# A decoder layer on one core: the first layer of the feed-forward net as rounded products, two couplings laid out by DMA, new call lists

## The chip, the core and the metric

The kernel runs on one core of a Trainium2 chip. A core has five engines with an instruction stream of their own: TensorE (PE in the profile, with PEld for its weight loads), VectorE (DVE), ScalarE (ACT), GpSimd (POOL) and SyncE (SP, here only the issuer of DMAs). They meet at semaphores: an instruction, or the landing of a DMA, raises one, and another engine waits until it has reached a value. The metric is the device time of one execution in microseconds (us), lower is better; the median of the runs is compared.

## What is computed

A decoder layer over 64 sequences of 256 tokens with 256 features, in fp32: a Mamba2 (SSD) mixer, an attention whose queries come from the sequence and whose keys and values come from 120 context rows and the sequence itself, a feed-forward net of three coupled cycles, each followed by a LayerNorm. The arithmetic to follow the change is that of the feed-forward net:

```python
def _coupling_net(h, w1, b1, w2, b2, w3, b3, w4, b4):
    h = _gelu(h @ w1 + b1)
    h = _gelu(h @ w2 + b2)
    h = _gelu(h @ w3 + b3)
    return jax.nn.sigmoid(h @ w4 + b4)
...
def _twist(x):
    o_r, o_i, p_r, p_i = jnp.split(x, 4, axis=-1)
    return jnp.concatenate([p_r, -p_i, -o_r, o_i], axis=-1)
global_context = x.mean(axis=1, keepdims=True)
gf = _global_net(global_context, gc_w1, gc_b1, gc_w2, gc_b2, gc_w3, gc_b3)
out = x
for _ in range(NUM_CYCLES):
    tf = _coupling_net(out, cn_w1, cn_b1, cn_w2, cn_b2, cn_w3, cn_b3, cn_w4, cn_b4)
    combined = 0.7 * gf + 0.3 * tf
    coupling = BASE_COUPLING + adaptive_range * (combined - 0.5) * 2.0
    out = out + coupling * _twist(out)
```

The rest in one line each:

```python
x = _layernorm(x + _L0_attn_ref(x, ...), axis=-1)             # mixer
x = _layernorm(x + _L0_xattn_ref(ctx_1024, x, ...), axis=-1)  # attention, 8 heads of 64
x = _layernorm(x + _L0_ffn_ref(x, ...), axis=-1)              # 256-256-128-64-1 net, three cycles
```

A coupling is one number for each token. The twist mixes features only, so after two cycles of couplings c and d the output is a sum of x, twisted x and sign-changed parts with factors of c, d and the last coupling e. The kernel uses this twice: cycles 1 and 2 apply the net's first layer to x and to twisted x once (`layer(f, 0, 0)` and `twisted(f)`) and then only combine the results, and the output is formed from x2 with the factors of_x, of_tw and of_minus.

## The kernel before

**Stages.** A sequence is 2 x 128 tokens or 2 x 128 features; 128 is the partition count. The work is a software pipeline. In pass p of `for p in range(NSEQ + 2)` the mixer and the start of the attention work on sequence m = p, the rest of the attention on a = p − 1, the feed-forward net on f = p − 2, and projections of sequence m + 1 begin already. There are 66 passes; 62 hold work of all of f, a, m and m + 1.

**Order.** Each engine runs a list of calls written out by hand, one in the prologue and one in the pass: `tensor` (L467 and the list after it), `scalar`, `vector`, `gpsimd`, `sync`. A call emits a few instructions for one sequence and does nothing where the sequence doesn't exist. Nothing is reordered: an instruction whose semaphore hasn't come holds all that follows on its engine. For SP that holds for its waits too: `keep_inv` and `spread_inv` stand between `load_x`, `load_ctx`, `spread_cum` and `store`.

**PSUM.** Eight banks: scores in 1 to 3, a ring of 4 and 5 (transposed probabilities, values, w_o), a ring of 6 and 7 (mixer projections, `glob`, `twisted`), and bank 0 for the feed-forward net.

**Products.** `product3` (L233, its matmul at L239) is the product of operands that were split into a half rounded to F32R and the rest: three rounds, high by high, low by high, high by low; each is one PE instruction for 128 rows of the contraction. The mixer's projections, `q_pair` (12 of 256 columns), `k_tile` (6 of 376) and `v_tile` (6 of 512) use it. A plain fp32 matmul shows as two PE instructions in the trace: `layer(f, 0, 0)` (L480) and `twisted` (L529, L530) have four matmuls each.

**Feed-forward net.** `x2_turn` (PE, L467) transposes x2; ScalarE's `x2_out` copies it to x2T and sums the tokens; `layer(f, cyc, n)` for n = 0 to 3 alternates a product on PE with a gelu or tanh on ScalarE; `cycle(f, cyc)` on VectorE turns the tanh of all tokens, replicated over partitions, into couplings cpl (L1233) and updates h_pre (L1243, L1245), of which the next cycle's gelu is taken. GpSimd's `twist` forms what the second cycle adds. For the output the couplings are needed a second time, with the token on the partition: `layer(f, cyc, 3)` makes them with a two-column product (L500) behind the two products that replicate (L499), and ScalarE takes a tanh of each (L811 and L813); GpSimd's `factors` makes of_x, of_tw and of_minus of them for `out_sum` on VectorE (L1254).

**Attention's division.** `inverse(a, d)` on VectorE makes the inverses of the softmax sums for head group d. SP's `keep_inv(a, d)` (L1600) writes them to DRAM in four DMAs and `spread_inv(a, d)` (L1610) reads them back replicated over 64 partitions into invT in two; `divide(a, d)` (L1193) multiplies oT with it, and `w_o(a, i)` (PE, L455) projects the result.

**Prologue.** `x_low(0)` (L985) is what TensorE's first product waits for; the context of sequence 0 is loaded behind the weights by `load_ctx(0)` (L1617), and its statistics, `context(0)`, come later on VectorE.

## Time and profile before

| | value |
|---|---|
| median of three runs | 3988.45 us (3987.41 to 3992.45) |
| the profiled execution's own time | 3988.01 us |
| its span (first to last instruction) | 3986.1 us |
| mean granted clock of TensorE | 0.988 |
| PE busy | 3893.1 us, 98% |
| ACT busy | 3265.0 us, 82% |
| DVE busy | 3013.3 us, 76% |
| POOL busy | 1700.7 us, 43% |

The time is that of the whole execution, the span that of the recorded instructions in it. "Busy" is the time in which an engine has an instruction under way, summed over the span; DMA issues, branches and semaphore operations are not counted as busy. The granted clock is TensorE's as a share of its upper level. In a timeline each row is a run of like instructions: start, duration until the last of them ends, engine, line, operation and operands. Matmuls overlap, so the duration of a group on TensorE's own time is read from its start to the start of the next row.

### The profile page before, as it was taken

The numbers are of one execution on the slowest core, as the hardware profiler recorded it, in microseconds if no ns is written. First come the engines' busy times: TensorE is split into PE (matmuls) and PEld (weight loads), VectorE is DVE, ScalarE is ACT, GpSimd is POOL, SyncE is SP. The second block draws the span as 40 slices with busy tenths as digits, with TensorE's granted clock in tenths as the row PEclk, the third lists the DMA queues.
The fourth block names the chain that finished last, engine by engine and source line by source line (L and its number), as shares of the span: only waits on it lengthen the run. The fifth ranks groups of instructions, "written<-read, shape, count | busy, mean of one in ns | idle before, by whom it ended". The sixth has DMA issues, their size and how long they took to land.

```text
span 3986.1 us, 75957 instructions
## 1 busy us (share of the span) xinstructions
PE 3893.1 (98%) x25728; PEld 3057.0 (77%) x25728; DVE 3013.3 (76%) x7082; ACT 3265.0 (82%) x7932; POOL 1700.7 (43%) x2824
## 2 busy tenths in 40 slices
PE   5999999999999999999999999999999999999995
PEld 4777777777777777777778777777777777777774
DVE  6777777877877877877777777777778778778763
ACT  4788888888888888888888888888888888888873
POOL 3344444444444444444444443444444444544431
PEclk7999999999999999999999999999999999999997
DMA  3111111211111111111111111111112111112100
GB/s 96 50 41 56 59 41 53 62 41 53 59 43 53 59 44 53 54 49 53 48 55 53 44 59 53 41 57 57 41 53 62 41 53 59 43 53 59 44 30 14
DMA packets 276722, 202.78 MB, mean 51 GB/s; under 512 B 19824, under 2 KB 275568, under 8 KB 276336
## 3 DMA queue, kind: packets, MB, share of 16 engines
q1 hardware_dynamic: 276336, 197.92, 16.4%
q8 instruction: 207, 3.39, 0.4%
q14 instruction: 179, 1.47, 0.1%
HBM read 180.04 MB, written 17.83 MB: 50 GB/s over the span
## 4 chain that ended last, share of the span: by engine, by line
PE 95%; DVE 1%; ACT 1%; issue 0%; POOL 0%; POOLq 0%; DVEq 0%; ACTq 0%
PE psum L239 29%; PE psum L420 10%; PE psum L444 9%; PE psum L430 9%; PE psum L455 6%; PE psum L330 5%; PE psum L487 5%; PE psum L317 5%; PE psum L480 3%; PE psum L493 3%; PE psum L499 2%; PE psum L529 2%; PE psum L530 1%; PE psum L304 1%; PE psum L467 1%; PE psum L363 1%
## 5 line engine op out<-in xcount | busy, mean ns | idle before, releaser
L762 ACT ACTIVATE prob<-psum,nmax 128x376 f32<-128x376 f32 x1024 | 587.9, 575 | 20.5 <-DVE nmax L1165 3.9
L1438 POOL TENSOR_TENSOR Lm<-Lm,G 128x768 f32<-128x768 f32 x256 | 468.4, 1837 | 265.5 <-ACT Lm L699 265.4
L1165 DVE TENSOR_REDUCE nmax<-psum 128x1 f32<-128x376 f32 x1024 | 544.5, 542 | 37.1 <-PE psum L420 28.3
L1428 POOL TENSOR_SCALAR_AFFINE_SELECT Lm<-Lm 128x256 f32<-128x256 f32 x512 | 218.2, 455 | 767.8 <-DMA Lm<-cum_row 767.8
L430 PE MATMUL psum<-ident,prob 128*128 128x128 f32 (+1 forms) x3072 | 490.7, 276 | 3.1 <-ACT prob L762 2.0
L989 DVE SCALAR_TENSOR_TENSOR u<-psum,par,u 128x255 f32<-128x255 f32 (+5 forms) x960 | 449.4, 479 | 34.2 <-ACT u L640 3.6
L420 PE MATMUL psum<-kT,q_sb 64*128 64x376 f32 x2048 | 462.8, 528 | 2.2 <-ACT kT L743 0.5
L430 PEld LDWEIGHTS psum<-ident,prob 128*128 128x128 f32 (+1 forms) x3072 | 366.8, 141 | 91.5 <-issue 61.3
L1184 DVE COPY probT<-psum 128x384 f32<-128x384 f32 x512 | 278.4, 544 | 178.9 <-PE psum L430 178.0
L444 PE MATMUL psum<-probT,V 128*64 128x256 f32 (+1 forms) x3072 | 386.8, 386 | 0.4 <-ACT V L752 0.4
L239 PE MATMUL psum<-x_hi,w_in_hi 128*128 128x256 f32 (+1 forms) x1152 | 350.3, 304 | 22.2 <-DVE x_lo L985 13.0
L772 ACT ACTIVATE probT<-psum 128x384 f32<-128x384 f32 x512 | 250.6, 489 | 94.1 <-PE psum L430 91.7
L239 PE MATMUL psum<-x_hi,w_in_lo 128*128 128x256 f32 (+1 forms) x1152 | 326.3, 283 | 0.0
L239 PE MATMUL psum<-x_lo,w_in_hi 128*128 128x256 f32 (+1 forms) x1152 | 325.4, 282 | 0.0
L444 PEld LDWEIGHTS psum<-probT,V 128*64 128x64 f32 (+1 forms) x3072 | 200.8, 136 | 105.7 <-issue 22.4
L698 ACT ACTIVATE Lm<-Lm,ncum 128x256 f32<-128x256 f32 x512 | 262.8, 513 | 0.8 <-POOL Lm L1428 0.8
L239 PEld LDWEIGHTS psum<-x_hi,w_in_hi 128*128 128x128 f32 (+1 forms) x1152 | 215.0, 187 | 57.2 <-issue 46.8
L420 PEld LDWEIGHTS psum<-kT,q_sb 64*128 64x128 f32 x2048 | 155.0, 185 | 117.5 <-issue 100.6
L804 ACT ACT_TABLE_LOAD x188 | 241.2, 1283 | 3.3
L762 ACT ACT_TABLE_LOAD x187 | 239.9, 1283 | 3.3
L1447 POOL TENSOR_TENSOR g<-xc,gate 128x256 f32<-128x256 f32 x256 | 190.5, 754 | 122.0 <-DVE xc L1083 93.5
L330 PE MATMUL psum<-w_out_sb,g 128*128 128x256 f32 x1024 | 231.7, 380 | 1.7 <-DVE dt_a L1001 1.7
(203 smaller groups left out, 10692.5 us busy)
## 6 DMA issues: line engine op xcount, KB each, us to landing
Lm<-cum_row SPq DMA_DIRECT2D x64, 1024.0 KB, 5.2
Lm<-cum_row SPq DMA_DIRECT2D x64, 512.0 KB, 6.5
invT<-inv_row SPq DMA_DIRECT2D x256, 128.0 KB, 3.0
xT_sb<-in_xT SPq DMA_DIRECT2D x64, 256.0 KB, 2.9
x_sb<-in_x SPq DMA_DIRECT2D x64, 256.0 KB, 3.4
result<-out_sb SPq DMA_DIRECT2D x64, 256.0 KB, 2.2
inv_row<-inv_t SPq DMA_DIRECT2D x512, 1.0 KB
ctx_sb<-in_ctx SPq DMA_DIRECT2D x64, 120.0 KB, 3.2
```

The source lines that it names most:

```text
L239: t = mm(dst, a, b, start=n == 1, stop=n == 3 * KT)
L330: t = mm(banks[b][:, i * D:(i + 1) * D], g[:, c, i * P:(i + 1) * P], w_out_sb[:, c, :], start=c == 0, stop=c == CT - 1)
L420: mm(banks[b][:, 0:NK], q_sb[r, c, i * P:(i + 1) * P], kT[r, c, :], start=True, stop=True).then_inc(p_sc, 1)
L430: t = tr(banks[b][0:m, j * P:(j + 1) * P], prob[:, r, j0:j0 + m], ident[:, :])
L444: t = mm(banks[b][k * HD:(k + 1) * HD, 0:L], V[0:m, j, h * HD:(h + 1) * HD], probT[0:m, (8 * s + h) % HP, j, :], start=j == 0, stop=j == l ...
L698: act(Lm[:, h, 0:L], Lm[:, h, 0:L], ACT.Exp, bias=ncum[:, 0, h:h + 1])
L762: act(prob[:, r, :], b[:, 0:NK], ACT.Exp, bias=nmax[:, n:n + 1], accum_out=psum_row[:, n:n + 1]).then_inc(a_exp, 1)
L772: act(probT[:, (8 * s + 2 * c + k) % HP, :, i * P:(i + 1) * P], b[:, 0:len(JT) * P].rearrange("p (j t) -> p j t", j=len(JT)), ACT.Copy).th ...
L989: stt(u[0:rows, c, d:L], src[:, 0:L - d], prm("conv_w", 4 * c + 3 - d, slice(0, rows)), u[0:rows, c, d:L], ALU.mult, ALU.add).then_inc(don ...
L1165: e.tensor_reduce(nmax[:, n:n + 1], banks[bank_of["sc", s, n]][:, 0:NK], AX.X, ALU.max, negate=True).then_inc(d_max, 1)
L1184: cp(probT[:, (8 * s + 2 * c + k) % HP, :, i * P:(i + 1) * P], b[:, 0:len(JT) * P].rearrange("p (j t) -> p j t", j=len(JT))).then_inc(d_tn, 1)
L1438: tt(pair, pair, G[:, :].unsqueeze(1).broadcast_to([P, 2, TRI]), ALU.mult).then_inc(l_Lm, 1)
```

## The change

Three things are changed.

First, `layer(f, 0, 0)` and `twisted(f)` are products of three rounds, like the mixer's. Their common operand x2T is split once, by a new VectorE call `x2_split(f)`: a cast to x2T_hi and a subtraction to x2T_lo. The weights are split in the prologue (cw1_hi, cw1_lo and the negated cw1_mhi, cw1_mlo). x2T becomes an alias of h_pre, and h_tw is gone: `twist` now works in place in h_a and h_b and waits until cycle 0 has used them.

Second, only cycle 2 makes its coupling in token order by the two-column product. Those of cycles 0 and 1 are brought to c_col by DMA: `keep_c` writes one row of cpl to DRAM, `spread_c` reads it with the token on the partition (128 partitions, 2 elements of 4 bytes each). Both are issued by SP, and `factors` waits for c_in. ScalarE's tanh of all tokens writes cpl itself, so t4 is gone. ctx_sb holds one sequence instead of two, so `load_ctx(s)` waits for all three uses of the sequence before (d_ctx), and the ring of prob tiles has 7 places instead of 8.

Third, all call lists are in another order, the prologue's too. There, `context(0)` is now ahead of `x_low(0)` on VectorE, and ctxT(0), in_z(0, 1) and y_pair(0, 0) move in front of the loop on TensorE.

```diff
 # tensor
             def layer(s, cyc, n):
...
                 if n == 0:
-                    pe.wait_ge(a_f, FA * s + 1)
+                    pe.wait_ge(set_dve, SET_DVE_ALL)
+                    pe.wait_ge(d_x2, 2 * s + 2)
                     for m in range(KT):
-                        for k in range(KT):
-                            t = mm(b[:, m * L:(m + 1) * L], cw1_sb[:, k, m * P:(m + 1) * P], x2T[:, k, :], start=k == 0,
-                                   stop=k == KT - 1)
+                        cs = slice(m * P, (m + 1) * P)
+                        t = product3(b[:, m * L:(m + 1) * L], [cw1_hi[:, k, cs] for k in range(KT)],
+                                     [cw1_lo[:, k, cs] for k in range(KT)], [x2T_hi[:, k, :] for k in range(KT)],
+                                     [x2T_lo[:, k, :] for k in range(KT)])
...
-                    for i in range(TT if cyc < 2 else 0):
-                        mm(b[:, i * P:(i + 1) * P], cw4_row[:, i, :], h3[:, :], start=True, stop=True)
-                    mm(b[:, L:L + TT], h3[:, :], cw4_col[:, :], start=True, stop=True).then_inc(p_f, 1)
+                    if cyc == 2:
+                        t = mm(b[:, 0:TT], h3[:, :], cw4_col[:, :], start=True, stop=True)
+                    else:
+                        for i in range(TT):
+                            t = mm(b[:, i * P:(i + 1) * P], cw4_row[:, i, :], h3[:, :], start=True, stop=True)
+                    t.then_inc(p_f, 1)
...
 # scalar
-                    sc.wait_ge(l_fac, 9 * s)
-                    t = act(t_col[:, cyc, :], src[:, 1, 0:TT], ACT.Tanh, bias=half_b4[:, :], scale=0.5)
-                    if cyc < 2:
-                        t = act(t4[:, :], src[:, 0, :], ACT.Tanh, bias=half_b4[:, :], scale=0.5)
+                    if cyc == 2:
+                        sc.wait_ge(l_fac, 8 * s)
+                        t = act(t_col[:, :], src[:, 0, 0:TT], ACT.Tanh, bias=half_b4[:, :], scale=0.5)
+                    else:
+                        sc.wait_ge(c_out[cyc], 16 * s)
+                        sc.wait_ge(l_tw, 2 * s)
+                        t = act(cpl[:, cyc, :], src[:, 0, :], ACT.Tanh, bias=half_b4[:, :], scale=0.5)
...
 # vector
+            def x2_split(s):
+                if not live(s):
+                    return
+                ve.wait_ge(a_f, FA * s + 1)
+                ve.wait_ge(p_f, FP * (s - 1) + 2)
+                ve.wait_ge(p_tw, s)
+                cp(x2T_hi[:, :, :], x2T[:, :, :]).then_inc(d_x2, 1)
+                ve.wait_ge(d_x2, 2 * s + 1)
+                tt(x2T_lo[:, :, :], x2T[:, :, :], x2T_hi[:, :, :].bitcast(F32), ALU.subtract).then_inc(d_x2, 1)
...
+            context(0)
             x_low(0)
...
+            split(cw1_raw, cw1_hi, cw1_lo)
...
 # sync
+            def keep_c(s, cyc):
...
+                sp.wait_ge(d_f, FD * s + 3 * cyc + 1)
+                sp.wait_ge(c_in[cyc], 16 * (s - 1))
+                e.dma_start(c_row[s % 2, cyc:cyc + 1, :], cpl[0:1, cyc, :]).then_inc(c_out[cyc], 16)
+
+            def spread_c(s, cyc):
...
+                sp.wait_ge(c_out[cyc], 16 * (s + 1))
+                sp.wait_ge(l_fac, 8 * s)
+                e.dma_start(c_col[:, cyc, :], c_row[s % 2, cyc, :].rearrange("(i p) -> p i", p=P),
+                            allow_slow_non_contiguous=True).then_inc(c_in[cyc], 16)
...
             for p in range(NSEQ + 2):
                 f, a, m = p - 2, p - 1, p
+                load_ctx(m + 1)
                 load_x(m + 1)
-                load_ctx(m + 1)
+                spread_cum(m + 1)
                 keep_inv(a, 0)
+                keep_inv(a, 1)
+                keep_c(f, 1)
+                keep_c(f, 0)
+                spread_inv(a, 1)
+                spread_c(f, 0)
+                spread_c(f, 1)
                 spread_inv(a, 0)
-                spread_cum(m + 1)
-                keep_inv(a, 1)
-                spread_inv(a, 1)
                 store(f)
```

The part of TensorE's new list on which the prediction works, from `twisted(f)` to the end of the pass, with twelve calls between `layer(f, 1, 3)` and `w_o(a, 0)`:

```python
layer(f, 0, 3), glob(f, 2), twisted(f), cb(m + 1), k_tile(m, 0), dcT(m + 1), q_pair(m, 0),
layer(f, 1, 1), scores(m, 0, 0), layer(f, 1, 2), turn(a, 14), in_z(m + 1, 0), layer(f, 1, 3),
turn(a, 15), k_tile(m, 1), xcT(m + 1, 0), scores(m, 0, 1), values(a, 3), k_tile(m, 2),
layer(f, 2, 1), turn(m, 0), xcT(m + 1, 1), layer(f, 2, 2), v_tile(m, 0), layer(f, 2, 3), w_o(a, 0)
```

On VectorE the new list has, from the second cycle on: `cycle(f, 1)`, `top(m, 1)`, `top(m, 2)`, `x_dt(m + 1, 0)`, `context_n(m + 1)`, `top(m, 3)`, `gate_silu(m + 1, 0)`, `divide(a, 0)`, `divide(a, 1)`.

TensorE at `twisted(f)`, in the order of the program, before (a row here is one matmul, which for fp32 is two instructions in the trace; cw is cw1, gw a weight of the global net):

```order
L514 MATMUL psum<-g,gw_sb 128x1
L529 MATMUL psum<-x2T,cw_minus 128x256
L530 MATMUL psum<-x2T,cw_sb 128x256
L529 MATMUL psum<-x2T,cw_minus 128x256
L530 MATMUL psum<-x2T,cw_sb 128x256
L517 MATMUL psum<-g,gw_row 128x1
L239 MATMUL psum<-kv_hi,wq_hi 128x256
L239 MATMUL psum<-kv_hi,wq_lo 128x256
```

and after:

```order
L530 MATMUL psum<-g,gw_row 128x1
L247 MATMUL psum<-x2T_hi,cw_mhi 128x256
L247 MATMUL psum<-x2T_hi,cw_mlo 128x256
L247 MATMUL psum<-x2T_lo,cw_mhi 128x256
L247 MATMUL psum<-x2T_hi,cw_hi 128x256
L247 MATMUL psum<-x2T_hi,cw_lo 128x256
L247 MATMUL psum<-x2T_lo,cw_hi 128x256
...
L302 MATMUL psum<-Cz,Bz 128x256
```

The four fp32 products have become twelve of three rounds (the six shown come twice), the last step of the global net stands ahead of them, and behind them the mixer's `cb` has taken the place of `q_pair`.

SP in a steady pass, before, from the loads to the inverses of group 1, with the semaphores waited for:

```order
L1576 DMA xT_sb<-in_xT 128x2x256 [waits d_x1p,d_xlo]
L1577 DMA x_sb<-in_x 128x2x256
L1617 DMA ctx_sb<-in_ctx 120x256 [waits d_ctx]
L1600 DMA inv_row<-inv_t 8x32 [waits inv_in0,d_inv]
L1600 DMA inv_row<-inv_t 8x32 x3
L1610 DMA invT<-inv_row 64x4x128 [waits d_o,inv_out0]
L1610 DMA invT<-inv_row 64x4x128
L1586 DMA cum_row<-dc 8x256 [waits cum_in,d_cum]
L1590 DMA Lm<-cum_row 128x8x256 [waits p_y,cum_out]
L1590 DMA Lm<-cum_row 128x8x128
L1600 DMA inv_row<-inv_t 8x32 [waits inv_in1,d_inv]
```

and after, from the inverses' writes to the store:

```order
L1639 DMA inv_row<-inv_t 8x32 [waits inv_in1,d_inv]
L1639 DMA inv_row<-inv_t 8x32 x3
L1658 DMA c_row<-cpl 1x256 [waits c_in1,d_f]
L1658 DMA c_row<-cpl 1x256 [waits c_in0]
L1649 DMA invT<-inv_row 64x4x128 [waits d_o,inv_out1]
L1649 DMA invT<-inv_row 64x4x128
L1666 DMA c_col<-c_row 128x2x1 [waits l_fac,c_out0]
L1666 DMA c_col<-c_row 128x2x1 [waits c_out1]
L1649 DMA invT<-inv_row 64x4x128 [waits inv_out0]
L1649 DMA invT<-inv_row 64x4x128
L1680 DMA result<-out_sb 128x2x256 [waits d_ffn1,d_ffn0]
```

The read of group 0's inverses has moved from right behind their writes to the end, behind the coupling's two writes, which wait for `cycle(f, 1)` (d_f), behind group 1's read and behind the coupling's two reads.

VectorE in the prologue, before, behind the split of w_in:

```order
L960 TENSOR_TENSOR w_in_lo<-Lm,w_in_hi 128x1104 [waits set_split]
L985 TENSOR_TENSOR x_lo<-xT_sb,x_hi 128x512 [waits a_xhi]
L989 SCALAR_TENSOR_TENSOR u<-psum,par,u 80x255 [waits a_uB]
L989 SCALAR_TENSOR_TENSOR u<-psum,par,u 80x254 [waits d_uB]
L989 SCALAR_TENSOR_TENSOR u<-psum,par,u 80x253 [waits d_uB]
```

and after:

```order
L984 TENSOR_TENSOR w_in_lo<-Lm,w_in_hi 128x1104 [waits set_split]
L992 BN_STATS st_ctx<-ctx_sb 120x6 [waits ctx_in0]
L995 BN_AGGR mv_ctx<-st_ctx 120x2 [waits d_ctx]
L1009 TENSOR_TENSOR x_lo<-xT_sb,x_hi 128x512 [waits a_xhi]
L1013 SCALAR_TENSOR_TENSOR u<-psum,par,u 80x255 [waits a_uB]
```

x_lo now stands behind two instructions of which the first waits for the landing of the context (ctx_in0).

## Rows read from the trace of the kernel before

**Rows 1.** Busy time by stretch, engines in the page's order, TensorE's clock, DMA share, GB/s

```profile
core 0: us, PE busy (x) PEld busy (x) DVE busy (x) ACT busy (x) POOL busy (x), PEclk, DMA share, GB/s
240.00:3720.00 3480.00, 3478.13 (x23197) 2737.49 (x23198) 2689.85 (x6342) 2945.48 (x7155) 1532.00 (x2545) 1.00 0.17 52
```

**Rows 2.** Timeline of TensorE, x2_turn in two passes (start us, us, engine, line, operation)

```profile
343.57 0.66 PE L467 MATMUL psum<-ident,x 128*128 128x128 f32 x4
...
3600.64 0.66 PE L467 MATMUL psum<-ident,x 128*128 128x128 f32 x4
```

**Rows 3.** Timeline of TensorE around layer(f, 0, 0) and twisted(f)

```profile
2036.26 1.99 PE L480 MATMUL psum<-x2T,cw_sb 128*128 128x256 f32 x8
2038.09 3.19 PE L330 MATMUL psum<-w_out_sb,g 128*128 128x256 f32 x14
...
2051.56 0.68 PE L529 MATMUL psum<-x2T,cw_minus 128*128 128x256 f32 x2
...
2053.37 0.28 PE L517 MATMUL psum<-g,gw_row 128*128 128x1 f32 x2
2053.51 0.36 PE L239 MATMUL psum<-kv_hi,wq_hi 128*128 128x256 f32 x1
...
2053.83 0.28 PE L239 MATMUL psum<-kv_lo,wq_hi 128*128 128x256 f32 x1
...
2055.00 0.33 PE L239 MATMUL psum<-kv_hi,wkv_hi 128*128 128x376 f32 x1
```

**Rows 4.** Timeline of TensorE, 2003 to 2017 us, the blocks around w_o

```profile
2003.91 1.52 PE L444 MATMUL psum<-probT,V 120*64 120x256 f32 x12
2005.36 0.71 PE L499 MATMUL psum<-h,cw_row 128*128 128x128 f32 x4
2005.91 0.28 PE L500 MATMUL psum<-cw_col,h 128*128 128x2 f32 x2
2006.05 0.42 PE L239 MATMUL psum<-kv_hi,wkv_hi 128*128 128x376 f32 x1
...
2007.17 0.28 PE L239 MATMUL psum<-kv_hi,wq_hi 128*128 128x256 f32 x1
...
2011.85 0.59 PE L239 MATMUL psum<-wkv_hi,kv_hi 128*120 128x512 f32 x1
...
2013.43 1.03 PE L487 MATMUL psum<-h,cw_sb 128*128 128x256 f32 x4
2014.39 0.90 PE L420 MATMUL psum<-kT,q_sb 64*128 64x376 f32 x4
2015.22 0.71 PE L493 MATMUL psum<-h,cw_sb 128*128 128x128 f32 x4
2015.77 0.60 PE L304 MATMUL psum<-ident,xc 128*128 128x128 f32 x4
...
2016.53 0.28 PE L500 MATMUL psum<-cw_col,h 128*128 128x2 f32 x2
```

**Rows 5.** Timelines of ScalarE, VectorE, SP in one pass; landing of invT

```profile
2067.35 0.48 ACT L813 ACTIVATE t<-psum,half_b 128x256 f32<-128x256 f32 x1
...
2066.66 0.69 DVE L1193 TENSOR_TENSOR oT<-oT,invT 128x512 f32<-128x512 f32 x1 [0.44 <-ACT oT L781]
...
2067.86 0.41 DVE L1233 TENSOR_SCALAR cpl<-t,tf_gain,c_cyc 128x256 f32<-128x256 f32 x1 [0.51 <-ACT t L813]
...
2057.78 1.36 SPq L1600 DMA_DIRECT2D inv_row<-inv_t  x4
2060.02 1.24 SPq L1610 DMA_DIRECT2D invT<-inv_row  x2
...
invT<-inv_row SPq DMA_DIRECT2D x256, 128.0 KB, 3.0
```

**Rows 6.** Prologue: VectorE's x_low(0), SP's load_ctx(0) and its landing

```profile
12.18 0.68 DVE L985 TENSOR_TENSOR x_lo<-xT_sb,x_hi 128x512 fp32r<-128x512 f32 x1
...
13.86 0.64 SPq L1617 DMA_DIRECT2D ctx_sb<-in_ctx  x1
...
ctx_sb<-in_ctx SPq DMA_DIRECT2D x1, 120.0 KB, 4.2
```

More of the change, by code:

```diff
@@ L538, in _ @@
             in_x(0, 1)
+            cb(0)
             dcT(0)
             in_z(0, 0)
-            cb(0)
             xcT(0, 0)
             xcT(0, 1)
+            ctxT(0)
+            in_z(0, 1)
+            y_pair(0, 0)
             for p in range(NSEQ + 2):
                 f, a, m = p - 2, p - 1, p
-                in_z(m, 1)
-                turn(a, 2)
-                turn(a, 3)
-                scores(a, 1, 1)
+                k_tile(a, 3)
+                v_tile(a, 1)
                 v_tile(a, 2)
@@ L551, in _ @@
                 turn(a, 4)
-                y_pair(m, 0)
-                values(a, 0)
-                scores(a, 2, 0)
-                turn(a, 5)
+                scores(a, 2, 1)
                 y_pair(m, 1)
                 y_pair(m, 2)
-                ctxT(m)
-                turn(a, 6)
-                turn(a, 7)
                 y_pair(m, 3)
-                scores(a, 2, 1)
-                x2_turn(f)
-                turn(a, 8)
+                scores(a, 3, 0)
+                turn(a, 5)
@@ L565, in _ @@
                 bcdt(m + 1)
                 in_x(m + 1, 0)
-                turn(a, 9)
-                scores(a, 3, 0)
-                layer(f, 0, 0)
+                turn(a, 6)
+                x2_turn(f)
+                scores(a, 3, 1)
+                values(a, 0)
                 out_proj(m)
                 mean_square(m)
-                turn(a, 10)
-                scores(a, 3, 1)
-                layer(f, 0, 1)
-                turn(a, 11)
+                turn(a, 7)
+                turn(a, 8)
@@ L576, in _ @@
+                layer(f, 0, 0)
+                turn(a, 9)
                 glob(f, 0)
                 in_x(m + 1, 1)
+                turn(a, 10)
+                values(a, 1)
+                turn(a, 11)
+                x1T(m)
+                layer(f, 0, 1)
+                values(a, 2)
                 layer(f, 0, 2)
-                values(a, 1)
+                glob(f, 1)
+                turn(a, 12)
+                turn(a, 13)
                 layer(f, 0, 3)
-                x1T(m)
-                values(a, 2)
@@ L583, in _ @@
-                turn(a, 12)
-                glob(f, 1)
+                glob(f, 2)
                 twisted(f)
-                glob(f, 2)
+                cb(m + 1)
+                k_tile(m, 0)
+                dcT(m + 1)
                 q_pair(m, 0)
-                k_tile(m, 0)
-                turn(a, 13)
-                dcT(m + 1)
+                layer(f, 1, 1)
                 scores(m, 0, 0)
+                layer(f, 1, 2)
+                turn(a, 14)
                 in_z(m + 1, 0)
+                layer(f, 1, 3)
@@ L593, in _ @@
+                turn(a, 15)
                 k_tile(m, 1)
-                turn(a, 14)
+                xcT(m + 1, 0)
                 scores(m, 0, 1)
-                layer(f, 1, 1)
-                turn(a, 15)
-                cb(m + 1)
-                layer(f, 1, 2)
+                values(a, 3)
+                k_tile(m, 2)
+                layer(f, 2, 1)
                 turn(m, 0)
-                values(a, 3)
-                layer(f, 1, 3)
-                k_tile(m, 2)
+                xcT(m + 1, 1)
@@ L604, in _ @@
+                layer(f, 2, 2)
+                v_tile(m, 0)
+                layer(f, 2, 3)
+                w_o(a, 0)
+                turn(m, 1)
+                ctxT(m + 1)
+                scores(m, 1, 0)
+                in_z(m + 1, 1)
                 q_pair(m, 1)
-                w_o(a, 0)
+                scores(m, 1, 1)
+                turn(m, 2)
                 w_o(a, 1)
-                v_tile(m, 0)
-                layer(f, 2, 1)
-                scores(m, 1, 0)
-                layer(f, 2, 2)
@@ L611, in _ @@
-                xcT(m + 1, 0)
-                turn(m, 1)
-                layer(f, 2, 3)
-                k_tile(m, 3)
-                v_tile(m, 1)
-                xcT(m + 1, 1)
+                turn(m, 3)
+                y_pair(m + 1, 0)
+                scores(m, 2, 0)
         @block.scalar
@@ L906, in _ @@
+                x1_out(m)
+                values_out(a, 2)
+                layer(f, 0, 2)
+                bcdt_th(m + 1)
+                glob(f, 1)
+                layer(f, 0, 3)
+                conv_th(m + 1, 0)
+                glob(f, 2)
                 keep_b(f)
-                glob(f, 2)
-                exp(a, 14)
+                turn_out(a, 13)
+                k_out(m, 0)
+                layer(f, 1, 0)
+                cb_out(m + 1)
                 q_out(m, 0)
-                k_out(m, 0)
@@ L950, in _ @@
+                exp(m, 9)
         @block.vector
@@ L1547, in _ @@
                 gated(m, 3)
+                context(m + 1)
                 squares(m)
```

356 lines of the change are left out of this document (182 added, 174 removed).

## The prediction

> **What bounds the kernel now.** I read the busy times by stretch first. From 240 to 3720 us TensorE is busy 3478.13 of 3480 us at a granted clock of 1.00, that is at its upper level of 2.4 GHz, while VectorE has 2689.85, ScalarE 2945.48 and GpSimd 1532.00 us of work there [rows 1]. So in the steady part a change is worth what it takes from TensorE's list, less whatever TensorE newly waits for; what it does to the other three engines counts only through such waits. The first transposition of x2_turn recurs on TensorE's timeline at 343.57 and, 54 passes later, at 3600.64: one pass lasts (3600.64 − 343.57)/54 = 60.32 us [rows 2]. 62 of the 66 passes have all three stages in them, so 0.1 us on a pass is 6.2 us, and the ends of the program are counted apart.
>
> **Products that become cheaper.** On TensorE's timeline layer(f, 0, 0) is eight fp32 instructions from 2036.26 to the next group's start at 2038.09, 1.83 us; twisted(f) is eight more from 2051.56 to 2053.37, 1.81 us [rows 3]. Each becomes twelve F32R instructions of 256 columns. The same form stands right behind twisted in this trace: q_pair(m, 0) is twelve of them, from 2053.51 to 2055.00, 1.49 us [rows 3]. The saving is 1.83 − 1.49 = 0.34 and 1.81 − 1.49 = 0.32, together 0.66 us a pass. Which weights and data are multiplied does not alter the shape, so I take this term as good to 0.1.
>
> The row gives a ratio of 1.49/1.82 = 0.82. The Trainium skill ("FP8 and Floating Point Precision", section "TensorE Precision Notes") counts true FP32 as four passes of the array, by which three rounds would cost 0.75 of the fp32 product and save 0.91 us a pass, some 16 us more over the program than my sum has. The trace has the duration itself, so the sum goes by the row.
>
> **Couplings.** The two-column product with cw_col goes from two cycles. It takes 2005.91 to 2006.05 = 0.14 us [rows 4]; two of them are 0.28 us. ScalarE loses two small tanh, GpSimd some small factor work, neither of which is late for TensorE in the steady part. x2_split puts a cast and a subtraction of 512 columns on VectorE; the subtraction of that size took 0.68 us [rows 6]. 1.4 us a pass at most goes into VectorE's idle 790 us of 3480 (13.7 us a pass) [rows 1].
>
> **The new order of calls.** In the old list q_pair(m, 0) and k_tile(m, 0) stand next to each other; the new one has dcT between them. A group of F32R products starts slower than it goes on: the first two instructions of q_pair take 2053.51 to 2053.83 = 0.32 us, the ten behind them 1.17, 0.117 each [rows 3]. One more such entry costs 0.32 − 2 × 0.117 = 0.09; I take +0.08 a pass. The rest of the list holds the same calls. Sum of TensorE's own work: −0.66 − 0.28 + 0.08 = −0.86 us a pass, if nothing waits.
>
> **What may wait.** Three chains that had room are now tight. The tightest is what w_o(a, 0) needs. Before, the normalisation of oT waited last for ScalarE's copy of oT (0.44 us idle) and not for a DMA [rows 5]. Now SP stands through the couplings' writes before it brings the inverses of attention group 0. From the end of layer(f, 1, 3): tanh 0.48; cpl scaled on VectorE 0.41; two keep_c issues, by the four keep_inv issues in 1.36 us, 0.34 each, 0.68; spread_inv(a, 1) 1.24; two spread_c issues; half of spread_inv(a, 0), 0.62; its landing, 3.0 from issue; the two multiplications of oT, 0.69 for the first, 1.3 for both [rows 5]. The two spread_c issues have no row of their own kind (128 partitions, 4 bytes each). From below they cost what a write of a few rows costs, 0.34; from above what half of a spread_inv costs, 0.62. I take 0.48, since they touch as many partitions as the dearer one and move less. Sum 0.48 + 0.41 + 0.68 + 1.24 + 0.96 + 0.62 + 3.0 + 1.3 = 8.7, with five hand-overs of some 0.04 (2067.35 + 0.48 to 2067.86 is one) 8.9 us; 8.4 to 9.4 with the unsure terms.
>
> Beside it TensorE has, between the end of layer(f, 1, 3) and w_o(a, 0), by the starts in [rows 4]: k_tile 1.12, twice; scores 0.83; values(a, 3) 1.45; layer(f, 2, 1) 0.96; xcT and turn, 0.76 for the two, twice; layer(f, 2, 2) 0.55; v_tile 1.58; layer(f, 2, 3) 0.14: 9.3 us. So the middle is a slack of 0.4 us and the ends −0.1 and +0.9. In this there is no room for what stands before the multiplications on VectorE (three maxima, xdt, ctx_n and the gate between the scaled cpl and oT, while its operations in [rows 5] take 0.4 to 0.7 us each), which is why I do not count on zero.
>
> A second chain: the write of the coupling has to have landed before spread_c can issue. From the issue of the last of four inv_row writes (2057.78 + 1.02 = 2058.80) to the issue of the read that waits for them, 2060.02, is 1.2 us [rows 5]. keep_c for cycle 0 issues last, and the 1.24 us of spread_inv(a, 1) stand before the wait, so it is hidden. The Trainium skill ("DMA: Bandwidth & Descriptors", section "Anatomy of one DMA — SWDGE (gpsimd) path") gives some 2.0 us of fixed cost for one DMA, most of it the receipt of the write. By that figure SP would stand 0.4 us more here, and the whole program would end near 3983. The trace's 1.2 us is on this queue and decides the sum.
>
> A third chain: twisted, the copy to h_b, the first cycle's update and layer(f, 1, 1) follow one another with only cb, k_tile (1.12), dcT and q_pair (1.49) on TensorE between [rows 3, 4], so layer(f, 1, 1) may start a few tenths late in some passes.
>
> For all of them I put a stall of 0.25 us on a pass: about half of the 0.4 us by which the first chain falls short in some passes or exceeds in others, plus the third. This is a choice, not a row; its ends are 0 and 0.6 for this forecast, and beyond it stands a rival. Net: −0.86 + 0.25 = −0.61, taken as −0.60; times 62 is −37.2 us.
>
> **The ends.** In the prologue VectorE now does the context's statistics before x_low(0). x_low ran at 12.18; the context's DMA issues at 13.86 and takes 4.2 us to land, 18.06 [rows 6], and with the statistics (two short operations, 0.6 by an estimate from the 0.41 of [rows 5]) x_low starts near 18.7, 6.5 us late. TensorE's first product needs it. Some of that comes back, since the context is ready earlier and TensorE waited for it later; against that cw1 is split too. I take +5.5 (3 to 8). In the tail x2_split, 1.4 us, lies on the last sequence's chain, with its hand-over +1.5. Together +7.0.
>
> **Sum.** The profiled execution's span is 3986.1, its own time 3988.0, 1.9 more; the median of the three runs is 3988.45. 3986.1 − 37.2 + 7.0 + 1.9 = 3957.8. Predicted 3958 us, 0.8% faster.
>
> **Rivals.** *Nothing waits* (chance 0.24): the chain ends ahead of w_o in every pass, as its slack of 0.4 says on its face, and the prologue gets half back: 3986.1 − 62 × 0.86 + 4.5 + 1.9 = 3939. The products at the page's price would end on this side too, and there I give that rule 0.03 of the 0.24. Against it: no idle time at all is a lot to ask of a list that reorders every call on five engines.
>
> *w_o waits for the detour over DRAM* (0.15), the one on the slow side: SP's list serialises two couplings and two inverses, and if the small DMAs issue or land slower than the nearest rows, or VectorE reaches the multiplications late, TensorE stands at w_o(a, 0) in each pass. The gain is gone from a stall of 0.86 − 7/62 = 0.75 us: 0.61 more stall is still faster by 0.2%, above 0.88 it is slower by as much. At 1.1 us: 3986.1 + 62 × 0.24 + 7 + 1.9 = 4010. For it: 0.6 us of unsure issue time and a landing of 3.0 that is a median. Against it: ScalarE's and VectorE's idle shares, and that the deficit must be twice what my upper end of the chain gives.
>
> *Half way* (0.13): stall of 0.65, by a DMA write that takes 2.0 instead of 1.2 us or as much lateness on VectorE: 3986.1 − 62 × 0.21 + 8.9 = 3982, no change. *My forecast* has 0.48.
>
> **Range and chances.** A measurement of this kernel can tell 0.2%, 8 us, from no change. Faster: 0.48 + 0.24 = 0.72; same 0.13; slower 0.15. The range reaches from 3930 (nothing waits and the prologue hidden, with a term for cheaper products) to 3998 (the start of the slow side), and leaves about 2 in 10 out.
>
> **What would show it.** Right: TensorE's pass near 59.7 us; the twelve x2T products at 1.5 us each; VectorE's multiplications of oT now released by the DMA of invT; TensorE's first product with x_lo near 19.4 us instead of 12.9. Wrong: idle TensorE time of over 0.6 us a pass in front of w_o's first product with oT, or in front of layer(f, 1, 1) (h_pre on VectorE as releaser); x2T products at 1.37 or at 1.8; issues of spread_c over 0.62; a coupling write that lands after 2 us.

## The result

The changed kernel takes 3997.11 us (median of 20 runs, 3988.62 to 4003.43) against 3987.86 us before (20 runs, 3986.36 to 3992.45): a ratio of 1.002, 95% interval 1.0013 to 1.0027. I had forecast 3958 us, 0.8% faster, and the time lies at the upper end of the range. It is no gain, by a hair a loss, and the runs spread 15 us where those of before spread 6.

The profiled execution of the changed kernel has a span of 3988.9 us, 2.8 more than before. Busy time by stretch; the fourth row answers to [rows 1]:

```profile
core 0: us, PE busy (x) PEld busy (x) DVE busy (x) ACT busy (x) POOL busy (x), PEclk, DMA share, GB/s
0.00:60.00 60.00, 15.87 (x78) 13.72 (x78) 39.20 (x73) 18.16 (x37) 12.80 (x22) 0.79 0.38 121
60.00:120.00 60.00, 46.37 (x271) 35.42 (x272) 35.63 (x88) 31.47 (x78) 21.83 (x28) 0.87 0.12 38
120.00:240.00 120.00, 114.80 (x760) 89.19 (x759) 90.19 (x208) 88.33 (x220) 48.19 (x75) 0.97 0.17 49
240.00:3720.00 3480.00, 3433.49 (x23504) 2717.93 (x23504) 2870.61 (x6483) 2886.61 (x7007) 1575.36 (x2546) 1.00 0.18 52
```

Over the whole span TensorE is busy 3836.7 us, 56.4 less than the 3893.1 before. So the work did leave its list, at least the forecast's 62 × 0.86 = 53 us (the experiments below put it higher, at 1.19 us a pass). But it stands idle 3480 − 3433.49 = 46.5 us in the steady stretch, where it was 1.9 [rows 1]. And in the first 240 us it is idle 63.0 us; the same sum over the stretches before gave 45.9. 56.4 were saved, 44.6 and 17.1 came back as idle time, the tail makes up the rest.

The waits of TensorE say where (engine, line, what it waited for: total us, times, longest):

```profile
PE psum L463 <- DVE probT L1208: 49.4, 62, 2.2
PE psum L247 <- DVE x_lo L1009: 19.6, 1, 19.6
PE psum L302 <- DVE Cz L1040: 14.8, 3, 7.9
...
PE psum L325 <- DVE gate L1063: 12.7, 1, 12.7
...
PE psum L247 <- DVE x2T_lo L1238: 2.2, 1, 2.2
```

L463 is the product of `w_o`. One wait in each of 62 passes, 0.80 us each, makes up the idle time of the steady part: 58 of them, 45.4 us and each between 0.35 and 1.8, lie between 240 and 3720 us. A pass, by the first transposition of `x2_turn` in 54 passes as in [rows 2], lasts 60.08 us, where it lasted 60.32. VectorE's own list has the link before it: its multiplication of oT waits for the DMA of the inverses, where before it waited for ScalarE [rows 5].

```profile
DVE oT L1217 <- DMA invT<-inv_row: 119.6, 63, 5.2
2018.37 1.29 DVE L1217 TENSOR_TENSOR oT<-oT,invT 128x512 f32<-128x512 f32 x2 [1.66 <-DMA invT<-inv_row]
```

The second line is one pass on VectorE's timeline: it had done all that stands before the multiplications 1.66 us before the inverses came.

Here is that pass along the chain of waits that ended last (start, us, what; pieces under 0.1 us are left out):

```profile
2008.83 1.28 ACT L780
2010.13 0.54 ACT prob L780
2010.69 0.48 ACT cpl L834
2011.19 0.43 DVE cpl L1267
2011.64 0.21 SPq L1658
2011.90 0.25 SPq L1658
2012.25 0.58 SPq L1649
2012.87 0.62 SPq L1649
2013.58 0.55 SPq L1666
2014.18 0.47 SPq L1666
2014.69 0.58 SPq L1649
2015.32 2.96 DMA invT<-inv_row
...
2018.98 0.68 DVE oT L1217
2019.66 0.48 DVE probT L1208
2020.18 1.99 PE psum L463 x8
```

and TensorE's timeline at the same place, the end of `layer(f, 1, 3)` (its next row starts at 2010.44) and the wait:

```profile
2010.00 0.60 PE L512 MATMUL psum<-h,cw_row 128*128 128x128 f32 x4
2010.44 0.49 PE L438 MATMUL psum<-ident,prob 128*120 128x128 f32 x3
...
2019.28 0.28 PE L509 MATMUL psum<-cw_col,h 128*128 128x2 f32 x2
2020.18 1.99 PE L463 MATMUL psum<-wo_sb,oT 128*128 128x256 f32 x8 [0.62 <-DVE probT L1208]
```

The tanh, the two coupling writes (L1658), group 1's read (L1649), the two coupling reads (L1666), group 0's read, its landing, the two multiplications: this is the detour that the prediction had written out. Behind the multiplications stands a link it did not have, the copy of probT (L1208). It frees the PSUM bank that `w_o(a, 0)` takes.

### The profile page after: what moved, and what is told of

Read it like the earlier page. It is cut to its first block, busy times and chain, and to the rows that moved or that the text cites. A ratio compares the mean times of both kernels' runs of the same rounds, so it can differ in the third digit from the quotient of the medians.

```text
span 3988.9 us, 77174 instructions
## 1 busy us (share of the span) xinstructions
PE 3836.7 (96%) x25984; PEld 3029.0 (76%) x25984; DVE 3195.2 (80%) x7215; ACT 3184.6 (80%) x7739; POOL 1742.9 (44%) x2824
## 3 DMA queue, kind: packets, MB, share of 16 engines
q1 hardware_dynamic: 311408, 198.20, 17.1%
## 4 chain that ended last, share of the span: by engine, by line
PE 77%; SPq 6%; DMA 5%; DVE 5%; ACT 4%; issue 3%; POOL 0%; DVEq 0%; ACTq 0%; POOLq 0%
PE psum L247 26%; PE psum L428 9%; PE psum L438 8%; PE psum L452 7%; PE psum L463 6%; PE psum L338 6%; DMA invT<-inv_row 5%; PE psum L325 5%; PE psum L497 3%; SPq L1649 3%; PE psum L503 2%; ACT L780 2%; SPq L1666 2%; DVE oT L1217 1%; ACT prob L780 1%
## 5 line engine op out<-in xcount | busy, mean ns | idle before, releaser
L1189 DVE TENSOR_REDUCE nmax<-psum 128x1 f32<-128x376 f32 x1024 | 533.8, 537 | 121.0 <-PE psum L428 121.0
L1476 POOL TENSOR_TENSOR Lm<-Lm,G 128x768 f32<-128x768 f32 x256 | 490.3, 1915 | 255.0 <-ACT Lm L717 255.0
L1530 POOL TENSOR_TENSOR h_a<-h_a,cpl 128x512 f32<-128x512 f32 x64 | 89.0, 1390 | 679.5 <-DVE h_pre L1275 679.5
L1208 DVE COPY probT<-psum 128x384 f32<-128x384 f32 x512 | 280.7, 548 | 68.1 <-PE psum L438 66.1
L463 PE MATMUL psum<-wo_sb,oT 128*128 128x256 f32 x1024 | 252.7, 391 | 51.7 <-DVE probT L1208 49.4
L1466 POOL TENSOR_SCALAR_AFFINE_SELECT Lm<-Lm 128x256 f32<-128x256 f32 x512 | 205.0, 434 | 101.4 <-DMA Lm<-cum_row 101.4
L463 PEld LDWEIGHTS psum<-wo_sb,oT 128*128 128x128 f32 x1024 | 187.3, 193 | 78.2 <-DVE probT L1208 54.7
```

The lines of the kernel that those rows point to most:

```text
L463: t = mm(banks[b][:, 0:D], oT[:, c, i * P:(i + 1) * P], wo_sb[:, c, :], start=c == 0, stop=c == CT - 1)
L1189: e.tensor_reduce(nmax[:, n:n + 1], banks[bank_of["sc", s, n]][:, 0:NK], AX.X, ALU.max, negate=True).then_inc(d_max, 1)
L1208: cp(probT[:, (8 * s + 2 * c + k) % HP, :, i * P:(i + 1) * P], b[:, 0:len(JT) * P].rearrange("p (j t) -> p j t", j=len(JT))).then_inc(d_tn, 1)
L1476: tt(pair, pair, G[:, :].unsqueeze(1).broadcast_to([P, 2, TRI]), ALU.mult).then_inc(l_Lm, 1)
```

## Experiments

My theory: the inverses of group 0 come to oT by way of SP's new list, and the end of this chain, plus the copy behind it, sets `w_o(a, 0)` in every pass. Rivals: VectorE is late by its own added work; the couplings' way to `factors` holds something; the gain on TensorE was never there. The times of before in these runs are 3987.5 to 3988.0 us; ratios are against it.

**All inverses ahead of the couplings on SP.**

```diff
                 keep_inv(a, 0)
+                spread_inv(a, 0)
                 keep_inv(a, 1)
+                spread_inv(a, 1)
                 keep_c(f, 1)
                 keep_c(f, 0)
-                spread_inv(a, 1)
                 spread_c(f, 0)
                 spread_c(f, 1)
-                spread_inv(a, 0)
```

> The changed kernel with one edit in SP's list: both reads of the inverses stand right behind their own writes again, ahead of the couplings' writes and reads. In the changed kernel's trace TensorE waits 49.4 us in 62 passes, 0.80 a pass, before w_o(a, 0), and VectorE waits 119.6 us in 63 for the DMA of invT before it multiplies oT. Theory 1 (the detour of the inverses behind the couplings sets w_o): both waits vanish, and the time falls by about 50 us, to 3945 to 3950. Rival 2 (VectorE is late by its own added work and by the copy that stands behind the multiplications): the wait on the DMA goes but w_o still waits for the copy of probT, under 15 us gained. Rival 3 (the couplings then come late to GpSimd's factors, and out_sum holds VectorE): a new wait of VectorE for of_minus, and the gain is under half.

Measured: 3927.38 us (3924.83 to 3930.62), ratio 0.9849 (0.9834 to 0.9863), 70 us below the changed kernel, more than the 50 expected. The two profiled executions are 63.5 us apart (spans 3988.9 and 3925.4): a pass is 59.18 us instead of 60.08, 56 us in 62 passes, and 8 us are gained outside them. The rest of the 70 comes from the changed kernel's profiled execution, whose own time of 3990.73 us is 6.4 under its median. The steady stretch, busy times as above:

```profile
240.00:3720.00 3480.00, 3477.05 (x23875) 2757.60 (x23874) 2921.07 (x6584) 2928.46 (x7114) 1599.04 (x2586) 1.00 0.18 52
```

and what is left of TensorE's wait before `w_o`:

```profile
PE psum L463 <- DVE probT L1208: 3.0, 3, 1.4
```

The wait is gone with nothing but four calls in another order on an engine that computes nothing. VectorE has the same work as before the edit, so its load was not the cause. The four runs also spread only 6 us again.

**The copy ahead of the multiplications on VectorE.**

```diff
+                turn_out(m, 0)
                 divide(a, 0)
                 divide(a, 1)
-                turn_out(m, 0)
```

> The changed kernel with one edit in VectorE's list: turn_out(m, 0), the copy that frees the PSUM bank which w_o(a, 0) takes, stands before the two multiplications of oT instead of behind them. In the trace w_o(a, 0) starts at the end of that copy, 0.5 us behind the end of the multiplications. Theory 1 (the DMA of invT sets the multiplications, and the copy adds itself behind): VectorE does the copy in the 1.66 us in which it waits for the DMA, w_o starts 0.48 us earlier and the time falls by 62 x 0.48 = 30 us, to about 3967; a wait of some 0.3 us a pass stays, now released by oT. If the bank were not what w_o waits for, nothing changes (within 5 us). If VectorE's load were the cause, the copy only shifts and nothing changes either.

Measured: 3971.11 us (3966.39 to 3972.07), ratio 0.9954 (0.9937 to 0.9971), 26 us below the changed kernel. The wait that stays has changed its name to the other thing `w_o` needs:

```profile
PE psum L463 <- DVE oT L1217: 36.5, 63, 2.5
```

So both hold `w_o`: the copy, for 0.42 us a pass between the medians and 0.27 by the passes of the profiled executions (60.08 and 59.82), and the DMA for the rest. The wait that stays, 36.5/63 = 0.58 us, is longer than the 0.3 expected.

**Context statistics later in the prologue.**

```diff
 # vector, prologue
-            context(0)
             x_low(0)
...
             conv(0, 3)
+            context(0)
 # gpsimd, prologue
-            context(0)
             masked(0, 0)
             times_g(0, 0)
             masked(0, 1)
+            context(0)
```

> The changed kernel with the statistics of the first context moved back behind conv(0, 3) on VectorE and behind masked(0, 1) on GpSimd, in the prologue only. In the trace of the changed kernel TensorE's first product starts at 19.64 us, before at 13.01. Theory: the first product is back near 13.0, and of the 6.6 us between 4 to 6.6 reach the end, 3991 to 3993. Rival: the prologue is bound further on (TensorE waits 12.7 us for the gate at 49 us, 7.9 for Cz), the shift is absorbed there and the time stays within 2 us of the changed kernel's.

Measured: 3992.46 us (10 runs, 3990.37 to 3999.13), ratio 1.0014 (1.0005 to 1.0024): 4.7 us below the changed kernel, with a spread of 9, so by itself no more than a hint. TensorE's first wait is 13.0 us again, and its idle time in the first 240 us is 59.2 us instead of 63.0. The next kernel has the same edit where the pass doesn't vary.

**All three edits.**

> The three edits together: inverses first on SP, the copy ahead of the multiplications on VectorE, context statistics later in the prologue. Theory 1: the stall of 0.80 us a pass is gone whole (the two edits overlap, so it is 50 us and not 80), and the prologue gives 4 to 6: 3937 to 3943, that is 1.1 to 1.3% faster than the kernel before. If only TensorE's own work set the pass then, the pass would be 60.05 - 0.80 = 59.25 us. Rival: the next wait takes over (h_pre for the feed-forward layers, or out_sum waiting for the couplings), and the pass stays over 59.6 us, 3955 or more.

Measured: 3921.85 us (3921.29 to 3927.79), ratio 0.9838 (0.9823 to 0.9852): 5.5 us less than with the first edit alone, and 15 under what I expected, since the first edit alone had given more. Of the 5.5, the prologue gives 4 to 5: idle time in the first 240 us falls from 63.4 to 59.0. The three waits before `w_o` that the first edit had left, 3.0 us, are gone too. TensorE's steady stretch is as full as before the change:

```profile
240.00:3720.00 3480.00, 3478.84 (x23891) 2758.88 (x23889) 2914.10 (x6589) 2930.62 (x7121) 1601.63 (x2589) 1.00 0.18 53
```

Of the waits that the rivals named, one is there, on GpSimd:

```profile
POOL cd L1544 <- DMA c_col<-c_row: 194.0, 64, 9.0
```

GpSimd waits 3 us a pass for the couplings' DMA, but TensorE stands only 1.2 of 3480 us idle, so this reaches nobody who matters. A pass is 59.13 us, against 60.32 before [rows 2]. It is the fastest kernel of this study, 1.6% faster than before.

**The parts of the change one by one**, undone in that kernel, in which nothing else waits. First the products as plain fp32 again:

```diff
-                        t = product3(b[:, m * L:(m + 1) * L], [cw1_hi[:, k, cs] for k in range(KT)],
...
+                        for k in range(KT):
+                            t = mm(b[:, m * L:(m + 1) * L], cw1_hi[:, k, cs].bitcast(F32), x2T_hi[:, k, :].bitcast(F32),
+                                   start=k == 0, stop=k == KT - 1)
```

(and `twisted` likewise).

> The kernel with the three edits (inverses first on SP, copy ahead of the multiplications, context later; 3921.85 us, pass 59.13 us, TensorE 3478.84 of 3480 us busy), with layer(f, 0, 0) and twisted(f) computed as plain fp32 products again, four matmuls each. x2_split stays; the products read the high halves alone, so the low part is left out of the result. Nothing else waits in that kernel, so this gives the first part of the change by itself. By the block times in the two traces (x2T products 3.62 us a pass in the kernel before, 3.03 in the one with three edits) the pass becomes 0.59 to 0.66 us longer: 62 x 0.62 = 38 us, 3958 to 3963. If three rounds cost three quarters of the fp32 product the difference would be 0.91 a pass, 3978. Rival: part of it is hidden or the switch between fp32 and rounded products costs as well, under 25 us.

Measured: 3960.30 us (3959.16 to 3960.71), ratio 0.9931 (0.9915 to 0.9948). The products are worth 38.4 us, 0.62 a pass; the pass itself grows from 59.13 to 59.73, by 0.60.

Then the couplings of all cycles by the two-column product and no DMA for them, `factors` as in the kernel before:

```diff
+                    for i in range(TT if cyc < 2 else 0):
+                        mm(b[:, i * P:(i + 1) * P], cw4_row[:, i, :], h3[:, :], start=True, stop=True)
+                    t = mm(b[:, L:L + TT], h3[:, :], cw4_col[:, :], start=True, stop=True)
...
-                keep_c(f, 1)
-                keep_c(f, 0)
-                spread_c(f, 0)
-                spread_c(f, 1)
```

> The kernel with the three edits, and the second part of the change undone: the couplings of cycles 0 and 1 are made in token order by the two-column product and a small tanh again, and the DMAs of the couplings are gone. TensorE's list gets 2 x 0.14 us for the products; in the traces the two cw_row products ahead of them also took 1.10 us a pass before against 0.89 after, so the pass should become 0.29 to 0.50 us longer: 3940 to 3953. If the DMAs disturb others by their traffic in the kernel with three edits, their removal gives some of that back and the time stays under 3937.

Measured: 3948.93 us (3947.52 to 3950.92), ratio 0.9904 (0.9889 to 0.9919): 27.1 us, 0.44 a pass, more than the 0.28 of the two-column products alone. The pass itself grows by 0.38, to 59.51. TensorE's timeline at one of the restored products reads

```profile
1990.81 0.60 PE L509 MATMUL psum<-h,cw_row 128*128 128x128 f32 x4
1991.25 0.28 PE L510 MATMUL psum<-cw_col,h 128*128 128x2 f32 x2
```

so the products that replicate the tanh last 0.44 us with it behind them, as without it. And both undone at once:

> Both parts undone, in the new lists with the three edits (the low part of x2T left out of the result as above): what is left against the kernel before is the order of calls, x2_split, the buffers and the prologue. I had put the new order at +0.08 us a pass of TensorE's own work. If the sum of the parts holds, the pass is 59.13 + 0.62 + 0.40 = 60.15, and the time 3985, the kernel before within 0.1%. If the order itself gained (the traces put -0.2 to -0.3 us a pass on transpositions and the blocks beside them) it is under 3977. Rival: the parts do not add, because the last small product hides behind another, and it comes out under 3970.

Measured: 3987.31 us (10 runs, 3984.90 to 3989.69), ratio 0.9998 (0.9989 to 1.0008). The parts add up: 38.4 + 27.1 = 65.5, and 3987.31 − 3921.85 = 65.5. By the passes it is 0.60 + 0.38 + 0.21 = 1.19. The new lists with the three edits are in sum worth nothing against the old ones: a pass of this kernel is 60.10 us, 0.21 less than before, which is 13 us in 62 passes, and its ends are some 12 us longer.

**Only the couplings' reads behind the inverses**, from the changed kernel:

```diff
                 spread_inv(a, 1)
+                spread_inv(a, 0)
                 spread_c(f, 0)
                 spread_c(f, 1)
-                spread_inv(a, 0)
```

> The changed kernel, with only the couplings' two reads (1.06 us of issue) put behind the read of group 0's inverses on SP; both writes and their wait for cycle(f, 1) stay ahead of it. A part of the detour is taken away where the first experiment took all of it. Theory (w_o ends when the chain ends, beyond what TensorE has to do meanwhile): the chain gets 1.06 shorter; the full removal gave 70 us in 62 passes, 1.13 a pass, so nearly all of the stall goes and the time is 3927 + 62 x 0.07 = 3931, up to 3940 as the DMA's landing varies between passes. Rival: what counts is that SP waits for cycle(f, 1) at all; then under 30 us are gained, 3967 or more.

Measured: 3929.85 us (3927.45 to 3932.34), ratio 0.9856 (0.9841 to 0.9870). Taking 1.06 us from the chain gave 67 of the 70 us. SP's wait for `cycle(f, 1)` is harmless; it is the length that counts.

**The detour made longer**, from the changed kernel:

```diff
                 spread_c(f, 1)
+                more(f)          # three writes of one row of constants to DRAM
                 spread_inv(a, 0)
```

> The changed kernel with three more small DMA writes (one row of 256 constants to DRAM, which nobody reads or waits for) issued by SP between the couplings' reads and the read of group 0's inverses, in each pass. They move nothing else and cost SP's time alone: a write of one row took 0.24 us at the median in the changed kernel's trace (c_row), so the detour becomes 3 x 0.24 to 3 x 0.29 = 0.7 to 0.9 us longer. Theory (in the changed kernel the detour sets w_o in every pass, one for one): 3997 + 62 x 0.8 = 4047, between 4040 and 4055, 1.3 to 1.7% slower than the kernel before. If something beside the detour holds w_o as well, or only in some passes the detour is last, the time rises by less than 25 us. The same slope taken the other way, 1.06 us less, had stopped at 67 us because the chain then ended ahead of TensorE.

Measured: 4076.40 us (4067.29 to 4076.80), ratio 1.0215 (1.0198 to 1.0232): 79 us above the changed kernel, where 43 to 58 were expected. The three writes take 0.90 us on SP's timeline:

```profile
2058.78 0.90 SPq L1666 DMA_DIRECT2D pad<-ones  x3
```

TensorE's wait before `w_o` over the program:

```profile
PE psum L465 <- DVE probT L1210: 111.0, 62, 3.3
```

The wait rose by 111.0 − 49.4 = 61.6 us, 0.99 a pass. From the first of the couplings' reads to the read of group 0's inverses SP now takes 2.06 us instead of 1.11: 0.95 more, nearly one for one, as the theory has it. Between the two profiled executions the span rose by 4074.6 − 3988.9 = 85.7 us, so 24 us are not waiting. In the longest of the passes TensorE's timeline reads

```profile
708.28 0.28 PE L511 MATMUL psum<-cw_col,h 128*128 128x2 f32 x2
711.81 3.78 PE L465 MATMUL psum<-wo_sb,oT 128*128 128x256 f32 x8 [3.25 <-DVE probT L1210]
715.38 0.85 PE L440 MATMUL psum<-ident,prob 128*120 128x128 f32 x3
```

and the window from 711.5 us on (busy times, then the clock)

```profile
711.50:716.50 5.00, 4.69 (x13) 3.62 (x13) 1.69 (x4) 0.00 (x0) 1.32 (x7) 0.50 0.00 0
```

while an ordinary pass has

```profile
649.23 1.99 PE L465 MATMUL psum<-wo_sb,oT 128*128 128x256 f32 x8 [1.58 <-DVE probT L1210]
```

With the wait of 3.25 us the granted clock falls to 0.50 (from 711.1 us, still inside the wait, to 717.9), the lower level of 1.2 GHz, and the eight matmuls of `w_o` take 3.6 us to the start of the next row where they take 1.83 behind a wait of 1.58. 14 of 56 steady passes have such a slow first group of `w_o` (2.3 to 3.6 us), and last 62.6 to 65.5 us where the median of the others is 60.9. In all the clock is at 0.50 for 51 us of the steady stretch; at half speed that costs 26 us by this estimate, about the 24 that were missing.

## Why the prediction was wrong

**The bound** was read rightly: TensorE's list and its waits set the pass in every kernel here.

**Products that become cheaper**: forecast 0.66 us a pass, measured 0.60 by the passes and 0.62 between the medians (38.4 us). Right. The Trainium skill's count of four passes for fp32 ("FP8 and Floating Point Precision", section "TensorE Precision Notes") would have given 0.91; the measured ratio is that of the row, 0.83, not 0.75.

**Couplings**: forecast 0.28, measured 0.38 by the passes and 0.44 between the medians (27.1 us). The two-column products are the 0.28 that I priced: in the kernel that has them back they take 0.29 us a pass more. The other 0.1 is spread over the starts of other groups, up to 0.08 us a pass each and of either sign; what sets them was not shown. It is not in the products that replicate the tanh: these take 0.44 us here and took 0.55 before (2005.36 to 2005.91 [rows 4]), but they take 0.44 in the new lists with the two-column product behind them too, so that gain belongs to the order.

**The new order**: forecast +0.08. With both parts undone and the stall taken out the pass is 60.10 against 60.32, so −0.21. That is a sum of larger terms of both signs: the 128-row transpositions of probabilities take 3.53 us a pass there and took 4.16, `w_o` takes 3.54 and took 3.27. Together TensorE's own work fell from 60.32 to 59.13, by 1.19 us a pass and not 0.86. With no stall the kernel would have beaten the forecast by far.

**What may wait**: this step failed. I forecast 0.25 us a pass and gave 0 to 0.6 as its ends. Measured it is 0.95 by the passes of the profiled executions (60.08 against 59.13); the profile calls 0.80 of it a wait, since it counts from the modelled end of the last product, 0.14 us behind the moment at which the next could start. The 70 us of the first experiment, 1.13 for each of 62 passes, hold more than the stall of the pass: 8 us outside the passes, and 6 by which the profiled execution is under the median. The first chain was the right one, link by link, and my arithmetic put it at 8.9 us against 9.3 of TensorE's work. In the trace it takes 2010.44 to 2019.66, 9.2 us, to the end of the multiplications; TensorE's work up to `w_o` ends at 2019.42, 9.0 us. Two errors of 0.3 us each had already used up the slack of 0.4. With the copy behind the multiplications the chain is 9.74 us, and 9.74 − 8.98 = 0.76 is this pass's stall. So two more things made the stall:

- The copy of probT behind the multiplications. `w_o(a, 0)` needs a bank as well as oT, and I followed only the data. I had read VectorE's new list as far as `divide(a, 1)`; the next call in it is `turn_out(m, 0)`. The second experiment prices it at 0.3 to 0.4 us a pass.
- The landing. I used its median, 3.0 us, for a chain with no slack left. In the kernel before, the same DMA took 2.9 to 4.6 us, in the changed one the time from the issue to the multiplication goes from 2.9 to 4.2 us, and the wait of TensorE at `w_o` from 0.35 to 1.8 us, longer where the landing is. Where there is slack such a spread costs nothing. Here the median wait of the steady passes is 0.67 us and the mean 0.78, so in this execution the late landings cost 0.1 us a pass, less than the copy. The spread of the runs goes the same way: 15 us over 20 runs of the changed kernel, 6 and 5 us over 4 runs each of the two kernels that only take the inverses, or part of the detour, out of the way. But late landings are not all of it: TensorE's mean granted clock is 0.986 to 0.988 in the six shortest of the 20 and 0.984 in the four longest (the last section comes back to this). How much is either was not seen, since only one execution is profiled.

The rest of the chain was as forecast: spread_c 0.53 each where I took 0.48 between 0.34 and 0.62 (for a reason that doesn't hold: it touches 128 partitions, half of a spread_inv 64), 1.24 for a pair of spread_inv, the tanh not delayed by more than 0.1 us by the exp and the table load ahead of it on ScalarE. The coupling's write was hidden, as said, behind spread_inv(a, 1), and its landing is the 1.2 us of the row I took or less: in the changed kernel each of the 128 writes has raised its semaphore fully 1.06 to 1.17 us after its issue. In the kernel with three edits, where the two reads of group 1's inverses are issued just ahead of it, it takes 1.1 to 2.4 us, and SP waits for it in every pass, here at the long end, 2.2 us after the second write:

```profile
1981.19 0.69 SPq L1658 DMA_DIRECT2D c_row<-cpl  x2
1983.80 0.90 SPq L1666 DMA_DIRECT2D c_col<-c_row  x2
```

The Trainium skill's some 2.0 us of fixed cost ("DMA: Bandwidth & Descriptors", section "Anatomy of one DMA — SWDGE (gpsimd) path", so for another path of issue) is near the second and not near the first. The prediction was right to go by the row.

The third chain cost nothing: between 240 and 3720 us TensorE has no wait over 0.4 us but those at `w_o`, and none before `layer(f, 1, 1)`.

**The ends**: forecast +7.0, and mis-sized too: in the profiled execution they are 3988.9 − 3986.1 + 62 × 0.24 = 17.7 us longer. TensorE's first product came at 19.64 us instead of 13.01, as worked out, and the edit that undoes it gives 4 to 5 us. But the idle time of the first 240 us rose by 17.1, and 13 of these stay when that edit is made: they belong to the rest of the prologue's new order. Among them are the three waits for Cz, 14.8 us, which the kernel before doesn't have; the one for the gate, 12.7 us, was 11.0. I priced one move in the prologue and left the others at nothing. The wait for x2T_lo in the tail is 2.2 us, where I had 1.5.

**The rivals.** "w_o waits for the detour over DRAM" is what happened, with its place and its mechanism, and near its price: it had 0.75 to 1.1 us of stall, and 0.95 was measured. I gave it 0.15 because the deficit had to be "twice" my upper end of the chain. That sentence was wrong by the prediction's own figures: the upper end, 9.4 against 9.3 us, is a deficit of 0.1, so a stall of 0.75 lay far outside the chain as I had drawn it, and it took the errors named above to reach it.

**The sum again**, with what was measured in the profiled executions: 3986.1 − 62 × 1.19 + 62 × 0.95 + 17.7 = 3988.9, the span, where the ends are the remainder; 1.9 more is its time, and the median is 6.4 above that. Against the forecast, 20 us too little gain from the work stand against 43 too little stall, 11 too little at the ends and the 6 of the profiled execution. That the time still came out only 1% above the forecast is in part luck, two errors of opposite sign.

## What to carry to other kernels

When a change puts a chain through another engine's queue, list all that the waiting instruction needs: its operand, its PSUM bank, and what stands on the engines that release each. Then compare the chain with the work beside it at its slow end too, with the largest landing and not only the median. If the slack that comes out is smaller than the sum of the roundings, forecast the stall and not half of it. And a DMA that many wait for belongs ahead of a DMA that nobody is waiting for: four calls in another order on SP turned a change that gained nothing into one that gains 1.5%.

## What the runs showed of the hardware

A wait of TensorE can cost more than its length, when the granted clock falls with it. In the kernel with the longer detour the clock stayed at 1.00 with a wait of 1.58 us and `w_o` took 1.83 us. With one of 3.25 us it was 0.50, and the pass paid for that on top of the wait. In all, 14 of 56 steady passes had it, with waits of 1.73 to 3.25 us. The length of the wait alone doesn't decide: of the 25 waits between 1.73 and 2.21 us, 13 came with a fall of the clock and 12 didn't.

In the profiled execution of the changed kernel, with steady waits of 0.35 to 1.8 us, it never happened. In that of the kernel with only the context statistics moved, whose passes have the same calls, it happened twice, with waits of 1.79 and 1.74 us; these two passes last 62.7 us instead of 59.8 to 61.5:

```profile
1419.00 3.06 PE L463 MATMUL psum<-wo_sb,oT 128*128 128x256 f32 x8 [1.79 <-DVE probT L1208]
2324.15 3.67 PE L463 MATMUL psum<-wo_sb,oT 128*128 128x256 f32 x8 [1.74 <-DVE probT L1208]
```

The lower mean clock of the changed kernel's longest executions, up to 4003 us, fits this; where in them the clock fell was not recorded.

The same small write to DRAM lands 1.1 us after its issue in one place of SP's list and up to 2.4 us in another, behind two larger reads. That the reads are the cause was not tested.
